# Masked softmax attention: adjacency turned in place into 32-bit codes in one GpSimd pass

## What is computed

```
h     = relu(layernorm(x))                       # x: 6144 x 128
score = h @ weight @ nodes.T                     # 6144 x 6144
score = where(adj > 0, score, -2**32 + 1)        # adj: int32, 6144 x 6144, some 4 ones a row
out   = x + softmax(score / 0.07, axis=1) @ nodes
```

## Time and profile before

| what | value |
|---|---|
| median of 3 runs | 926.37 us (925.98 to 926.46) |
| span of the profiled execution, first to last instruction | 922.5 us |
| the median less that span | 3.9 us |
| TensorE busy | 906.1 us, 98% |
| VectorE, ScalarE, GpSimd busy | 814.5, 744.0, 705.6 us |
| mean granted TensorE clock | 0.998 |
| read from HBM | 160.50 MB |

### The profile page before, as it was taken

The page is one execution under the profiler, slowest core; times in us unless marked ns, Lnnn a source line. Parts: engine busy times, 40 slices in busy tenths (PEclk is TensorE's granted clock), DMA queues, the critical chain, the costliest instruction groups (busy, mean ns, idle before and its releaser), DMA issues.

```text
span 922.5 us, 26099 instructions
## 1 busy us (share of the span) xinstructions
PE 906.1 (98%) x7566; PEld 659.9 (72%) x7566; DVE 814.5 (88%) x1626; ACT 744.0 (81%) x1468; POOL 705.6 (76%) x587
## 2 busy tenths in 40 slices
PE   7989999999999999999999999999999999999997
PEld 4466777777777777777777777777777777777776
DVE  6998889988998899889988998898889888988985
ACT  5987888888888888888888888888888888888885
POOL 5999878787778877887788778877887788788712
PEclk9999999999999999999999999999999999999999
DMA  9789999999999999999999999999999999999965
GB/s 343 232 224 257 279 267 278 257 287 266 286 278 267 272 273 273 267 272 273 276 273 267 269 274 274 275 260 276 276 268 265 276 274 278 260 270 269 278 105 100
DMA packets 360361, 242.46 MB, mean 263 GB/s; under 512 B 321808, under 2 KB 340368, under 8 KB 341904
## 3 DMA queue, kind: packets, MB, share of 16 engines
q1 hardware_dynamic: 353136, 238.87, 100.9%
q10 hardware_dynamic: 7200, 3.28, 1.5%
HBM read 160.50 MB, written 3.15 MB: 177 GB/s over the span
## 4 chain that ended last, share of the span: by engine, by line
PE 93%; DVE 2%; DMA 2%; SPq 2%; issue 1%; ACT 0%; DVEq 0%; ACTq 0%
PE ps_s L900 38%; PE ps_o L948 26%; PE ps_o L950 13%; PE ps_t L923 13%; DMA pT_dma<-split 2%; SPq L353 1%; PE ps_t L967 1%; DVE probs L695 1%; PE ps_s L977 1%; DMA nodes_raw<-in_L_gnn_input_dram 0%; DVE v L763 0%; DVE pT_lo L718 0%; DVE split L724 0%; PE ps_o L967 0%; DVE pT_hi L714 0%
## 5 line engine op out<-in xcount | busy, mean ns | idle before, releaser
L695 DVE CUSTOM_DVE_ANT_0 probs<-ps_s,absent 128x1024 f32<-128x1024 f32 x288 | 351.4, 1220 | 49.6 <-PE ps_s L900 42.8
L900 PE MATMUL ps_s<-yT_hi,hT 128*128 128x512 f16 x1152 | 389.2, 379 | 1.0 <-DVE chunk_max L695 0.9
L460 POOL TENSOR_SCALAR absent<-present 128x2048 bf16<-128x2048 bf16 x141 | 294.3, 2087 | 34.9 <-POOL present L451 34.3
L587 ACT ACTIVATE pT_hi<-ps_t 128x512 f16<-128x512 f32 x281 | 167.7, 597 | 156.0 <-PE ps_t L923 155.9
L451 POOL TENSOR_SCALAR present<-adj_i 128x2048 bf16<-128x2048 int32 x144 | 273.6, 1900 | 13.3 <-DMA adj_i<-in_adj_dram 13.3
L948 PE MATMUL ps_o<-v,pT_dma 128*128 128x256 f16 x1152 | 222.1, 273 | 5.2 <-DMA pT_dma<-split 2.9
L557 ACT ACTIVATE ps_t<-probs,neg_max,exp_scale 128x512 f32<-128x512 f32 x285 | 220.3, 773 | 2.6 <-DVE neg_max L705 1.2
L900 PE MATMUL ps_s<-yT_lo,hT 128*128 128x512 f16 x576 | 218.3, 379 | 0.0
L718 DVE TENSOR_TENSOR pT_lo<-ps_t,pT_hi 128x512 f16<-128x512 f32 x284 | 194.3, 684 | 21.8 <-ACT pT_hi L587 20.4
L948 PE MATMUL ps_o<-v,pT_hi 128*128 128x256 f16 x1152 | 205.9, 273 | 0.9 <-DVE pT_lo L718 0.8
L950 PE MATMUL ps_o<-v,pT_dma 128*128 128x128 f16 x1152 | 206.5, 220 | 0.0
(11 more groups left out here) (82 smaller groups left out, 508.8 us busy)
## 6 DMA issues: line engine op xcount, KB each, us to landing
adj_i<-in_adj_dram SPq DMA_DIRECT2D x144, 1024.0 KB, 5.3
pT_dma<-split SPq DMA_TRANSPOSE x288, 3.5
nodes_raw<-in_L_gnn_input_dram SPq DMA_DIRECT2D x6, 512.0 KB, 6.7
x_res<-in_x_dram SPq DMA_DIRECT2D x48, 64.0 KB, 3.9
out_dram<-fin ACTq DMA_DIRECT2D x48, 64.0 KB, 2.5
x_ln<-in_x_dram SPq DMA_DIRECT2D x46, 64.0 KB, 5.0
hT<-h_split SPq DMA_TRANSPOSE x45, 5.0
x_ln<-in_x_dram ACTq DMA_DIRECT2D x2, 64.0 KB, 3.0
```

The costliest lines, as they stand in the source:

```text
L460: nc.gpsimd.tensor_scalar(by_block(absent[:, c, :]), by_row(flags(s, c)), -ABSENT, ABSENT, ALU.mult, ALU.add).then_inc(absent_done, 1)
L587: nc.scalar.activation(pT_hi[:, p % BANKS, :], turn_area(k, at), ACT.Copy).then_inc(hi_done, 1)
L695: nc.vector.tensor_tensor_reduce(out=probs[:, s, j * SCORE:(j + 1) * SCORE], in0=ps_s[j % 2][:, :], in1=absent[:, c, part * SCORE:(part + ...
L900: made = nc.tensor.matmul(ps_s[j % 2][:, q * 512:(q + 1) * 512], hT[:, s, part, :], y[:, cols], start=(part == 0 and y is yT_hi), stop=(pa ...
```

## The change

GpSimd makes one pass over a chunk, in place: `adj * (-2^40) + 2^39`, written as uint32. A zero gives 2^39 and saturates at the largest uint32; a one gives a negative number and saturates at 0. VectorE subtracts this code in `mask`, read as uint32. The buffers `present` and `absent` and ScalarE's `early_absent` are gone, and so is the permutation: the nodes lie in natural order, so a node load reads 8 runs of 512 B for each partition where it read 2 runs of 2 KB. Scores are scaled down (`H_SCALE`, `Y_TOP`), so that they vanish beside the code of an absent neighbour. A buffer `adj_i[c]` is now free only when both masks of its chunk are done. Tile 1 has two buffers of its own for c = 0 and 1 (`adj_x`). The first load of `adj_i[2]` for tile 1, and those of tile 2, wait for masks, and stand in SP's order ahead of the first `turn_d`.

```diff
-    nodes_v = nodes.rearrange("(j g p b) d -> j p g (b d)", g=1024 // TURN, p=P, b=PER_TURN)
+    nodes_v = nodes.rearrange("(j b p) d -> j p b d", p=P, b=NODE_PART)
...
+            def next_adj(u, c):
+
+                sp.wait_ge(masked, u * SCORES + (PER_CONV * (c + 1) - SCORES * (2 if isinstance(u, int) and u == 2 and c < 2 else 1)))
+                load_adj(u, c)
...
             for c in range(CONVS):
                 load_adj(0, c)
             sp.dma_start(x_res[:, 0, :], x_v[0]).then_inc(x_res_in[0], 16)
+            for c in range(2):
+                load_adj(1, c)
             for u in range(2, 4):
                 sp.wait_ge(h_done, u - 1)
                 load_x(u, u % 2)
-            def early_adj(n):
-                sp.wait_ge(present_done, n + 1)
-                load_adj(n // CONVS + 1, n % CONVS)
-
-            for n in range(2 * CONVS - 1):
-                early_adj(n)
+            next_adj(1, 2)
+            for c in range(2):
+                next_adj(2, c)
...
             for g in range(2):
                 turn_d(0, 0, g, g + 1)
-            early_adj(2 * CONVS - 1)
...
                 for g in range(2):
                     turn_d(t, 2, g, late(at, 0, g) if at == LAST else evac(t, g - 2))
-                next_adj(0)
+                if has(at, 2):
+                    next_adj(t + 2, 2)
                 for g in range(2):
                     turn_d(t, 4, g, late(at, 1, g) if at == LAST else evac(t, 2 + g))
-                next_adj(1)
                 if has(at, 4):
                     sp.wait_ge(h_done, t + 3)
                     load_x(t + 4, par)
+                if has(at, 3):
+                    next_adj(t + 3, 0)
                 if has(at, 1):
                     for g in range(2):
                         turn_d(t + 1, 0, g, late(at, 2, g) if at == LAST - 1 else evac(t, 6 + g))
-                next_adj(2)
...
+                if has(at, 3):
+                    next_adj(t + 3, 1)
...
-                nc.gpsimd.tensor_scalar(flags(s, c), adj_i[:, c, :], 1.0, 0.0, ALU.min, ALU.max)\
-                    .then_inc(present_done, 1)
...
-                nc.gpsimd.tensor_scalar(by_block(absent[:, c, :]), by_row(flags(s, c)), -ABSENT, ABSENT,
-                                        ALU.mult, ALU.add).then_inc(absent_done, 1)
...
+                nc.gpsimd.tensor_scalar(codes(u, c), adjacency(u, c), PRESENT_STEP, ABSENT, ALU.mult, ALU.add)\
+                    .then_inc(coded, 1)
...
+            for c in range(2):
+                convert(1, c)
             v_lo_pool(0)
-            pool.wait_ge(absent_done, 4)
-            find_present(1, 1, 2)
-            make_absent(1, 1, 2, True)
+            convert(1, 2)
             make_h(2, 0)
-
-            find_present(2, 0, 0)
+            convert(2, 0)
             v_lo_pool(1)
-            find_present(2, 0, 1)
+            convert(2, 1)
             v_lo_pool(2)
...
-                    in0=ps_s[j % 2][:, :], in1=absent[:, c, part * SCORE:(part + 1) * SCORE],
+                    in0=ps_s[j % 2][:, :], in1=codes(u, c)[:, part * SCORE:(part + 1) * SCORE],
```

More of the change, by code:

```diff
@@ L184, in gnn_masked_attention_kernel @@
         adj_in = [sem(f"adj_in{i}") for i in range(CONVS)]
+        adj_x_in = [sem(f"adj_x_in{i}") for i in range(2)]
         stored = [sem(f"stored{i}") for i in range(2)]
@@ L188, in gnn_masked_attention_kernel @@
         half_done = sem("half_done")
[L189 to L192, removed]
+        coded = sem("coded")
         stats_done = sem("stats_done")
@@ L291, in turn_area, with adjacency, codes @@
             return ps_t[k % BANKS][:, :]
[L293 to L299, removed]
+        def adjacency(u, c):
+            return adj_x[:, c, :] if isinstance(u, int) and u == 1 and c < 2 else adj_i[:, c, :]
+        def codes(u, c):
+            return adjacency(u, c).bitcast(uint32)
         def has(at, ahead):
@@ L321, in load_adj @@
             def load_adj(u, c):
-                sp.dma_start(adj_i[:, c, :], adj_v[u][:, c * CONV:(c + 1) * CONV]).then_inc(adj_in[c], 16)
+                landed = adj_x_in[c] if isinstance(u, int) and u == 1 and c < 2 else adj_in[c]
+                sp.dma_start(adjacency(u, c), adj_v[u][:, c * CONV:(c + 1) * CONV]).then_inc(landed, 16)
+            def next_adj(u, c):
+                sp.wait_ge(masked, u * SCORES + (PER_CONV * (c + 1) - SCORES * (2 if isinstance(u, int) and u == 2 and c < 2 else 1)))
+                load_adj(u, c)
             sp.dma_start(w[:, :], weight).then_inc(w_in, 16)
@@ L436, in split_h, with convert @@
                     .then_inc(h_split_done, 1)
[L438 to L447, removed]
[L448 to L465 removed]
+            def convert(u, c):
+                if isinstance(u, int) and u == 1 and c < 2:
+                    pool.wait_ge(adj_x_in[c], 16)
+                else:
+                    pool.wait_ge(adj_in[c], u * 16 + (0 if c < 2 and not (isinstance(u, int) and u == 0) else 16))
+                pool.sem_inc(pool_waited, 1)
+                nc.gpsimd.tensor_scalar(codes(u, c), adjacency(u, c), PRESENT_STEP, ABSENT, ALU.mult, ALU.add)\
+                    .then_inc(coded, 1)
             def v_lo_pool(n):
@@ L518, in step @@
                     if at != 0:
-                        convert(t + 2, par, 1, True)
+                        convert(t + 2, 1)
                 if has(at, 3):
@@ L523, in step @@
                 if has(at, 2):
-                    convert(t + 2, par, 2, True)
+                    convert(t + 2, 2)
                 if has(at, 3):
-                    convert(t + 3, 1 - par, 0, True)
+                    convert(t + 3, 0)
                 if at == LAST - 1:
@@ L633, in step @@
                 for z in range(CYCLES):
-                    if at == 0 and z > 0:
-                        early_absent(2, z - 1)
                     hi_p(t, CYCLE * z, at)
```

54 lines of the change are left out of this document (9 added, 45 removed).

## The result

The changed kernel takes 1032.15 us (median of 4 runs, 1030.26 to 1034.67); the kernel before took 926.17 beside it (925.85 to 926.46). The ratio is 1.1152, with an interval of 1.1132 to 1.1171: slower by 106 us, where 7.2 were forecast. The span of the profiled execution is 1029.3 us.

The account below looks back on a forecast made before the run. TensorE was taken as the bound, at 18.3 us a step. Terms 1.1 + 1.1 + 5 = 7.2 on the profiled 922.5, plus 3.9 to the median, gave 933.6 us; range 924.5 to 944.

Parts of the forecast that it names:

- The steady steps: Steady loads move to masks, nearer the transposes in SP's order; landing 5.0 us, 0.3 to 1.2 to spare, cost 0.
- Rival B: Transposes come too late in every step: 0.2 us a step over 45 steps, 942.6 us; chance 0.10.
- GpSimd's pass: GpSimd's remaining single pass over a chunk takes 2.1 us (1.90 to 4.1), hidden behind TensorE, cost 0.
- VectorE's mask: VectorE's mask with its second operand grown from 2 to 4 bytes stays at 1.22 us, cost 0.
- The node loads: Six node loads at the start, in 512 B runs, end at 14.6 instead of 12.5 us: +1.1 (0 to +2.1).
- the queue behind it: Tile 1's first two chunks go ahead of tile 2's `x_ln`; `x_stats` waits until 27.5 us: +1.1 (0 to 1.5).
- Three loads ahead of the first transposes: At the start, three loads precede tile 0's transposes on SP; product 0 starts 4.1 us late: +5 (+2 to +7).
- rival D: Set-up hides it all, or late product 0 only fills the later gap: 926.4 us (924.5 to 928.2); chance 0.12.
- Rival E: Faster: GpSimd's L476 no longer meets `v_lo`, so product 4 starts up to 1.8 us sooner: 922.9 us; chance 0.12.

Follow-up runs that it names:

- the first two experiments: Changed kernel with each steady load behind its pair of transposes: 930.76 us; kernel before with only the steady loads' mask waits and places changed: 1026.58 us.
- the third experiment: Changed kernel, steady loads behind their pairs; at the start x rows precede tile 1's chunks, its third chunk follows tile 2's first two: 925.80 us.
- the second experiment: Kernel before, with only its steady adjacency loads waiting for masks and standing at the changed kernel's places in SP's order: 1026.58 us, ratio 1.1093.

## Why the prediction was wrong

The sign was right, and the size wrong by a factor of 15. The 1032.15 us lie outside the range of 924.5 to 944, and above the price of every rival, 982 at most.

**The step that failed is "The steady steps"**, which took 0. Rival B named the place but priced it at 0.2 us a step; it is 2.24. Two things in it were off, and a third that one might suspect was not.

1. *The landing.* I took 5.0 us, a figure that no row gave, and 0.3 to 1.2 to spare. The landing is 5.7. Product 8 uses its block 428.20 − 422.01 = 6.2 us after the issue, so with each pair issued on time 5.7 would still have left 0.5 us there: by this estimate the error alone comes to little or nothing at that place, and B is of that size.
2. *The issue.* I counted each pair's landing, and not how long SP is held in issuing it. "SP is not held up for long" is true of the waits for masks and false of the transposes. The earlier trace rows showed a second transpose whose issue lasted 3.38 us against 1.23 for the first. In the step shown the three pairs take 5.24 + 4.75 + 5.08 = 15.1 us of SP and all else, with the gaps, 20.59 − 15.1 = 5.5 us. With free pairs of 2.77 that is 13.8 us of 18.35; with pairs of 1.23 + 3.38 = 4.6 us, as in the earlier trace rows, it is 19.3, and already above the step. A sum over SP's queue would have found it, as the sum over GpSimd's passes found that engine free.
3. *The masks.* A loop through them offers itself: a load waits for a mask, the pair for the load, product 4 for the pair, and a later mask for product 4. In the changed kernel it does not bind. Mask (t+2, 1) ends at 456.93 and its load is issued at 458.36, only when SP comes to it, and in 480 us SP waits for masks twice, 2.1 us in all. The cycle closes in SP's queue alone: load at 458.36, pair at 459.05 held to 463.80, `hT`, residual rows, load at 466.12, pair at 466.78, and so on, with product 4 at 473.04 behind them. I treated each pair by itself, as if every pair started on time.

That the order of SP's issues is the cause is shown, from both sides, by the first two experiments. That SP's queue is the limit in the changed kernel is shown by its waits of 2.1 us in 480. The other kernels differ. SP waits 5.5 us in the same window with no load ahead of pair 4/5, so it is full there too. It waits for masks 36.7 us with no load ahead of pair 8/9 and 26.3 us with loads ahead of pair 8/9 alone, 24 times each, once a step: there masks do hold the queue, as in the loop of point 3. How each of these divides its loss between late landings and the loop stays open; the runs set the size of each place and not its share.

**GpSimd's pass.** Right: 1.91 us against 2.1 taken, no cost; GpSimd is busy for 416.8 us where 410 were forecast.

**VectorE's mask.** Right: 1.220 us, unchanged.

**The node loads.** Right in kind. The last lands at 14.9 us (14.6 forecast); in long runs they give 1.7 us back, give or take 1.0, against +1.1. VectorE's order brought what was forecast of **the queue behind it**: `x_stats` of tile 2 at 27.80 (27.5 forecast), waiting for `x_ln`.

```profile
27.80 0.29 DVE L631 BATCH_NORM_STATS2 stats<-x_ln 128x6 f32<-128x128 f32 x1 [1.14 <-DMA x_ln<-in_x_dram]
```

**Three loads ahead of the first transposes.** Right in mechanism; the places are a little later than forecast. SP and TensorE:

```profile
37.65 1.28 SPq L320 DMA_DIRECT2D adj_i<-in_adj_dram  x3
41.33 9.66 SPq L354 DMA_TRANSPOSE pT_dma<-split  x4
...
49.42 0.37 PE L900 MATMUL ps_o<-v,pT_dma 128*128 128x256 f16 x1 [5.00 <-DMA pT_dma<-split]
```

The three loads were forecast near 38 and product 0 at 49.0, after 4.5 us of idle time; it is 49.42 after 5.00. TensorE's clock is then 0.50, the lower level of 1.2 GHz, in the whole window from 49.20 to 55.00 shown above, where I took 3.3 us of it. The two changes of order in the third experiment, this one and `x_ln`'s, are worth some 5.0 us together, against 6.1 forecast, and the whole start 5.7 (3.4 to 8.0) against 7.2. That part of it runs while TensorE would have waited for `v_lo` anyway, as rival D has it, is argued and was not tried by itself.

**Rival E** was not borne out. In the third experiment the first transposes land at about 43.6, close to the 43 that E asks for, and the time is still level with the kernel before. GpSimd's pass and `v_lo` meet just as before, with a gap of 2.27 us behind them, as E's own "against" (49 to 52 again) says:

```profile
49.94 3.10 POOL L453 TENSOR_TENSOR v<-nodes_raw,v 128x1536 f16<-128x1536 f32 x1
...
51.20 2.38 DVE L715 SCALAR_TENSOR_TENSOR v<-nodes_raw,scale_bits,v 128x512 f16<-128x512 f32 x1
...
53.64 0.28 PE L900 MATMUL ps_o<-v,pT_dma 128*128 128x256 f16 x1 [2.27 <-DVE v L715]
```

The gain of 2.7 us over the kernel before came only with a further change, which took `v_lo` off VectorE.

## What to carry to other kernels

A buffer that is turned in place moves its next load from the first reader to the last one, and with it the place of that load in a serial DMA queue: ask what stands behind it there, and sum the queue's own issue time, held issues included, as for any engine. Here a 1 MB load issued 0.7 to 1.7 us ahead of a pair of transposes that the bound engine waits for held it up, and one issued 2.6 us ahead or more, directly behind the pair before, cost nothing. A queue with time to spare is not enough, though: with the loads on ScalarE's queue SP had some 100 us of 480 free, and the transposes still came too late. When such a row lasts longer than its neighbour (3.4 us for 1.2), read the row to its end before using its other number.

## What the runs showed of the hardware

- A DMA transpose lands 3.5 us (median) after its issue where no 1 MB load was issued less than 2.6 us ahead, 5.7 with one close ahead (5.8 in the second experiment), and 5.9 to 8.1 in the steps read with two, also when they were issued by ScalarE (7.3 to 7.9).
- The issue of the second transpose is held until the load ahead of it has landed: 1.23 us free, 3.2 with one load in the pair shown, 3.9 to 4.6 with two. The first of a pair is hardly held by one load (1.23 to 1.57 us in five pairs between 446 and 480 us), and behind two it took 1.30 to 2.39 us. Why it is the second was not tried.
- Node loads in runs of 512 B hold SP's queue too, where those of 2 KB did not the earlier trace rows. In the source line of the changed kernel the issue grows from 0.41 to 2.32 us:

```profile
L330 SPq DMA_DIRECT2D nodes_raw<-in_L_gnn_input_dram x6: 409/1444/2317, 1.2 to 7.6; - x6
...
DMA to landing us min/median/max: 4.7/7.3/7.9
```
